# TensorE marks graph 1 through the two PSUM banks of the column codes, and a round's second one-hot is issued behind the logits' maxima

## What is computed

```
# layer 0: of each node the first 25 neighbours by column; their elementwise maximum
vals, idx = top_k(where(A != 0, -arange(N), -inf), 25)
agg = max over the valid of X[idx];  agg = where(degree <= 25, maximum(agg, 0), agg)
x = layernorm(x + relu(concat([X, agg]) @ W + b))
# layer 1: attention of 8 heads over the neighbours
Wh = x @ W1;  e = leaky(s1[i] + s2[j] + emb[adj])  where adj, else -1e9
h = softmax(e) @ Wh;  x = layernorm(x + elu(layernorm(h) * gamma + beta))
```

## Time and profile before

| what | us |
|---|---|
| median of 3 runs (lowest, highest) | 3056.82 (3050.93, 3058.76) |
| the profiled execution | 3059.63 |
| its span | 3057.9 |
| VectorE busy | 2525.2 (83%) |
| GpSimd busy | 2208.5 (72%) |
| TensorE matmuls busy | 2007.9 (66%) |
| ScalarE busy | 1058.5 (35%) |

### The profile page before, as it was taken

One profiled execution on the slowest core, in us unless ns is written; L12 is line 12 of the kernel. 1 busy time (PEld: TensorE's weight loads), 2 busy tenths in 40 slices (PEclk: granted clock), 3 DMA queues, 4 the chain that ended last, 5 costly groups with the idle time before them and its releaser, 6 DMA issues.

```text
span 3057.9 us, 30468 instructions
## 1 busy us (share of the span) xinstructions
PE 2007.9 (66%) x6994; PEld 1423.7 (47%) x6995; DVE 2525.2 (83%) x5841; ACT 1058.5 (35%) x2587; POOL 2208.5 (72%) x2341
## 2 busy tenths in 40 slices
PE   8247566756666667766667667676677666477565
PEld 1134344534444445544455545554455444356453
DVE  6798887998888988889889988889896866577676
ACT  4223224333333333333443333333432222234334
POOL 3475567777777777777777777777777777777774
PEclk9968778777877788888888888887897887689787
DMA  8877667656666666766676666676655554445443
GB/s 300 258 229 227 205 213 220 187 171 191 203 184 207 189 195 209 216 208 188 205 218 193 195 205 217 190 220 193 198 156 143 158 147 132 128 134 170 128 134 91
DMA packets 282490, 577.75 MB, mean 189 GB/s; under 512 B 68801, under 2 KB 192706, under 8 KB 265922
## 3 DMA queue, kind: packets, MB, share of 16 engines
q0 software_dynamic: 109824, 305.79, 36.0%
q1 hardware_dynamic: 172482, 269.96, 26.4%
HBM read 488.78 MB, written 86.77 MB: 188 GB/s over the span
## 4 chain that ended last, share of the span: by engine, by line
POOL 43%; issue 18%; DVE 15%; PE 6%; DVEq 3%; DMA 3%; ACT 2%; POOLq 0%; ACTq 0%; SPq 0%
POOL ring L706 43%; DVE agg L1353 3%; DVEq L1126 3%; DVE pay L1172 2%; PE att_p L1016 2%; PE lin_p L979 1%; DMA ring<-nat_d,idx 1%; DVE ring L1492 1%; DVE agg L1344 1%; DVE pick L1230 1%; DVE adj_h L1159 1%; DMA ring<-table_d,top 1%; POOL pair_s L714 1%; PE score_p L952 0%; DVE lst L1251 0%
## 5 line engine op out<-in xcount | busy, mean ns | idle before, releaser
L706 POOL DMA_INDIRECT ring<-nat_d,idx x1096 | 1052.1, 960 | 390.6 <-issue 355.4
L706 POOL DMA_INDIRECT ring<-table_d,idx x1096 | 1046.2, 955 | 346.9 <-issue 332.0
L1016 PE MATMUL att_p<-ring,ident 128*128 128x256 f32 (+1 forms) x2384 | 575.2, 397 | 211.3 <-ACT x_t L809 125.6
L1016 PEld LDWEIGHTS att_p<-ring,ident 128*128 128x128 f32 (+1 forms) x2384 | 461.9, 198 | 327.4 <-issue 180.7
L1353 DVE TENSOR_REDUCE agg<-ring 128x256 f32<-128x2560 f32 (+9 forms) x120 | 473.1, 3942 | 2.7 <-issue 0.4
L979 PE MATMUL lin_p<-w_s,h_t 128*128 128x256 f32 x1024 | 428.9, 592 | 0.0
L979 PEld LDWEIGHTS lin_p<-w_s,h_t 128*128 128x128 f32 x1024 | 289.3, 296 | 123.1 <-issue 65.1
L837 ACT ACTIVATE neg<-z 128x256 f32<-128x256 f32 x128 | 53.3, 416 | 799.0 <-DVE z L1395 799.0
L1492 DVE TENSOR_TENSOR ring<-ring,score_p 128x1536 f32<-128x1536 f32 (+10 forms) x128 | 320.6, 2504 | 10.3 <-issue 1.0
L966 PE MATMUL turn_p<-ident,xs 128*128 128x128 f32 x256 | 65.5, 346 | 383.1 <-ACT h_t L802 365.0
L952 PE MATMUL score_p<-pay,pick 128*128 128x323 f32 x896 | 299.2, 482 | 18.9 <-DVE pick L1230 16.2
(11 more groups left out here) (193 smaller groups left out, 2868.8 us busy)
## 6 DMA issues: line engine op xcount, KB each, us to landing
adj_i<-in_adj_dram SPq DMA_DIRECT2D x128, 1024.0 KB, 5.7
sorted_d<-srt SPq DMA_DIRECT2D x112, 161.5 KB, 2.8
ring<-nat_d,idx POOLq DMA_INDIRECT x1096, 2.9
ring<-table_d,idx POOLq DMA_INDIRECT x1096, 2.9
table_d<-tab SPq DMA_DIRECT2D x128, 132.0 KB, 4.4
nat_d<-pay SPq DMA_DIRECT2D x32, 514.0 KB, 4.6
pay<-in_x_dram SPq DMA_DIRECT2D x32, 512.0 KB, 7.5
xs<-sorted_d SPq DMA_DIRECT2D x128, 128.0 KB, 4.1
```

The lines of the kernel that those rows point to most:

```text
L706: pool.indirect_dma_start(out=to[:, k * width:(k + 1) * width], out_offset=None, in_=source, in_offset=bass.IndirectOffsetOnAxis(ap=idx_at ...
L1016: last = pe.matmul(att_p[:, 0:C], ident[0:on, :], r3[0:on, s, 0:C], start=(s == 0), stop=(s == k - 1))
```

## The change

Graph 1's tiles (n = 16 to 31) are marked by TensorE as graph 0's are. Their slices use only two banks, those that hold the column codes later (`score` for n >= 16: bank c % 2), so a slice waits until VectorE has taken the maxima of the slice two before it (`score_free`). In the steps 16 to 22 TensorE does the four slices of tile n at the head of its step, ahead of `ranks` and the permutes. In rounds 0 to 8, slices 2 and 3 of tile r + 23 stand between TensorE's first permute and `turn(r)`, slices 0 and 1 of tile r + 24 at the end of its round. VectorE takes the maxima of slices 0 and 1 where `chunks` stood and of 2 and 3 where `mark(n+1)` stood. `cast(n)` waits for `score_ready` up to n = 33. The column codes wait in `res`, and VectorE copies them to PSUM in four pieces in round 8, ahead of `mark(32)`, instead of one copy in step 16. The constants for TensorE's marks move out of `ring` to `fin` and `turned_out`. `index_rows` decodes graph 1 as graph 0. In all rounds the second `pick_rows` is issued behind the maxima of the logits; in rounds without logits, behind x1.

```diff
-        parts_h = ring[0:64, 2 * N:2 * N + N // 2].bitcast(BF16)
-        mark_h = ring[:, 3 * N:3 * N + P // 2].bitcast(BF16)
-        cols_h = x1k[:, 0:N // 2]
+        parts_h = fin[0:64, :].bitcast(BF16)
+        mark_h = turned_out[0][:, 0:P // 2].bitcast(BF16)
+        cols_h = [res[c][:, :] for c in range(4)]
...
-            return score_banks[(4 * n + c) % BANKS]
+            return score_banks[(4 * n + c) % BANKS if n < T else c % 2]
+
+        def score_free(n, c):
+
+            return 4 * n + c - BANKS + 1 if n < T else 4 * T if n == T and c < 2 else 4 * n + c - 1
...
-                if n < T + 2:
+                if n < 2 * T + 2:
                     need(act, score_ready, 4 * (n - 1))
                 else:
-                    need(act, cast_used, n - 1 - T)
+                    need(act, cast_used, n - 1 - 2 * T)
...
-            def mark(n):
+            def mark(n, quarters=range(4)):
 
                 pe.wait_ge(cast_done, n + 1)
-                for c in range(4):
+                for c in quarters:
                     at = slice(512 * c, 512 * (c + 1))
-                    need(pe, score_used, 4 * n + c - BANKS + 1)
+                    need(pe, score_used, score_free(n, c))
...
             for n in range(AHEAD):
-                if n < T:
-                    mark(n)
+                mark(n)
...
-            pe.wait_ge(score_used, 4 * T)
+            mark(AHEAD, (0, 1))
...
                 if perms:
                     permute(perms[0])
+                if r + AHEAD < 2 * T:
+                    mark(r + AHEAD, (2, 3))
...
                     if first(r):
                         turn(r)
+                if r + AHEAD + 1 < 2 * T:
+                    mark(r + AHEAD + 1, (0, 1))
...
-                if first(n):
+                if n < 2 * T:
+                    search_first(n, (0, 1))
+                elif first(n):
                     chunks(n)
                 if r and ranked_in(r - 1) is not None:
                     rank_rows(ranked_in(r - 1))
-                for x in PERMS_OF[r]:
-                    pick_rows(x)
+                perms = list(PERMS_OF[r])
+                if perms:
+                    pick_rows(perms[0])
...
                     v.tensor_reduce(mx[:, :], e3.rearrange("p k h -> p h k"), AX, ALU.max)
+                if perms[1:]:
+                    pick_rows(perms[1])
+                if first(j):
                     settle()
                     v.tensor_tensor(e3, e3, mx[:, :].unsqueeze(1).broadcast_to([P, k, H]), ALU.subtract)\
                         .then_inc(logits_ready, 1)
...
-                if first(n + 1):
+                if n < 2 * T:
+                    search_first(n, (2, 3))
+                if n + 1 == 2 * T:
+                    settle()
+                    for c in range(4):
+                        v.tensor_copy(score_p[0][:, C * c:C * (c + 1)], cols_h[c])
+                    settle()
+                if 2 * T <= n + 1 < TILES:
                     mark(n + 1)
...
-                    v.tensor_copy(score_p[0][:, :], cols_h)
```

More of the change, by code:

```diff
@@ L75 @@
 CONSTS1 = 45
-CONSTS = 48
+CONSTS = 51
 ORDER1 = [6, 14, 11, 0, 2, 4, 13, 15, 1, 3, 5, 8, 10, 7, 9, 12]
@@ L683, in _ @@
             step(pool.tensor_scalar(cols_i, cols_i, 65536.0, None, ALU.mult))
-            step(pool.tensor_copy(cols_h.bitcast(BF16), ring[:, 0:N]))
+            for c in range(4):
+                step(pool.tensor_copy(cols_h[c].bitcast(BF16), ring[:, 512 * c:512 * (c + 1)]))
             assert steps == CONSTS
@@ L1173, in chunks, with search_first @@
                 last.then_inc(cast_used, 1)
[L1175 to L1182, removed]
+            def search_first(n, quarters=range(4)):
+                if quarters[0] == 0:
+                    free_pay(n)
+                for c in quarters:
                     dve.wait_ge(score_ready, 4 * n + c + 1)
@@ L1243, in index_rows @@
                 i3 = idx_part(b, part)
-                none = 0.0 if b else MARK
+                none = MARK if b < 2 else 0.0
                 rounds = [-(-SLOTS[at + u] // 8) for u in range(PART)]
@@ L1272, in index_rows @@
                 settle()
-                if b == 0:
+                if b < 2:
                     v.scalar_tensor_tensor(l3, l3, none, l3, ALU.is_gt, ALU.mult)
@@ L1521, in _ @@
                     degree_codes(n // GROUP)
[L1522 to L1525, removed]
+                search_first(n)
                 if n % GROUP == GROUP - 1:
@@ L1531, in _ @@
                     score_weights()
-            mark(AHEAD)
             settle()
```

## The result

| kernel | median us (lowest, highest) | runs | ratio to before, 95% interval | span of the profiled execution |
|---|---|---|---|---|
| before | 3056.82 (3050.93, 3058.76) | 3 | | 3057.9 |
| after | 3102.37 (3100.80, 3102.61) | 3 | 1.015 (1.0136 to 1.0164) | 3100.9 |

A forecast was written before the change was run, and what follows sets the result against it. VectorE's chain up to GpSimd's first layer-1 gather at 446 us was taken to bound the kernel. 8.3 - 1.0 + 38 + 2 - 2.4 = +45, less a little, +44 us: 3100 us, range 3072 to 3124.

The forecast's parts named there:

- the gather: GpSimd's first gather of layer 1, at 446 us before; expected near 490 us after the change.
- the ring: Rounds 1 to 7: slices, cast, `h_t`, `turn`, linear and VectorE's maxima wait in a closed cycle through three engines; +38 us.
- What bounds the kernel: Up to 446 us VectorE's work stands end to end; a microsecond there moves GpSimd's first layer-1 gather and the end equally.
- VectorE's saving: Per tile of graph 1, VectorE's product goes and maxima come out of PSUM: 0.94 us less a round, if TensorE is never late.
- The terms of the ring: Rounds 1 to 7: TensorE fp32 66 us, slices 22.7, ScalarE's casts, copies and tables, VectorE 18.7; 123 us after overlap and clock.
- Steps 16 to 22: Before round 0: TensorE's slices delay the permutes from step 20 on, and VectorE waits; +8.3 us, or +5.5 with 0.54 us slices.
- The moved one-hot: The second one-hot, issued later, saves VectorE's waits for permutes in rounds 10 and 14; -2.4 us.
- Whatever happens on the other engines there is covered.: From 446 us on GpSimd never stands still, so delays on other engines cost nothing until the last 30 us.
- The hidden ring: Rival: the next tile's slices 0 and 1 are always ready when VectorE needs them; -10 us, 3047 us, chance 0.08.
- No change: Rival: the loss ahead of the first layer-1 gather doesn't reach the end; 3057 us, chance 0.10.
- The upper clock throughout: Rival: TensorE runs at its upper clock throughout, rounds 1 to 7 take 100 us; sum +19, 3076 us, chance 0.22.
- the lower clock throughout: Rival: TensorE runs at its lower clock throughout, rounds 1 to 7 take 149 us; sum +71, 3128 us, chance 0.10.

The follow-up runs named there:

- ring_open: The changed kernel with slices 2 and 3 at the head of TensorE's round and slices 0 and 1 of the next tile ahead of `turn`; 3052.49 us.
- all_early: ring_open with the two permutes of step 21 put behind TensorE's marks of step 22; 3049.05 us, 0.9974 of before.
- slices23_early: The changed kernel with only slices 2 and 3 at the head of TensorE's round; on two other chips 3859.06 us (0.9958 of before there) and 3919.43 us (0.9991).

## Why the prediction was right, point by point

| stretch | predicted | measured |
|---|---|---|
| to the start of round 0 | +8.3 | +2.9 (149.65 against 146.78) |
| round 0 | -1.0 | -0.8 |
| rounds 1 to 7 | +38 | +40.2 |
| round 8 | +2 | +2.2 (12.8 against 10.6) |
| rounds 9 to the gather | -2.4 | -2.1 |
| behind the gather | 0 to -0.5 | +0.6 |
| span | +44 to +45 | +43.0 |

The start of round 0 is +2.9 against before; against the two repeats of its steps it is +6.2 and +3.4. As a single stretch is known to 3 or 4 us, the agreement of the entries of about 2 us and less shows nothing. That the median came within 2.4 us of the forecast is in part luck too: the 5.4 us too much ahead of round 0 and the 2.2 too little in the ring, whose own terms missed in both directions, took each other off.

- **What bounds the kernel.** Right for what lies ahead of the gather, and the step that carried the most: six kernels and one bare delay moved the gather by 6 to 44 us, and the end moved with it, within the few us by which the last column varies.
- **VectorE's saving.** 0.94 us a round was predicted; VectorE's busy time fell by 1.00 a round in ring_open and in all_early, the two kernels whose rounds show it with hardly a wait on slices (by 0.82 in after, where the waits hide it).
- **The ring.** Its links are the ones named: the cast on slice 3, `h_t` behind the cast, `turn` on `h_t`, slice 0 behind linear. Opening any of them gave time back, opening it in two places gave all of it. The signs asked for came too: 41.6 us of waits for slices in the seven rounds (30 or more), 57.3 us before seven casts, where it was 18.8, the gather at 488.7 (near 490).
- **The terms of the ring.** The sum hit, its parts less so. TensorE's groups of after in these rounds (174.8 to 299 us), to be read beside the earlier trace rows:

```profile
L984 PE MATMUL lin_p<-w_s,h_t 128*128 128x256 f32 x56 | 25.6, 638 | 0.0
L957 PE MATMUL score_p<-pay,pick 128*128 128x323 f32 x64 | 25.1, 547 | 8.2 <-DVE pick L1234 8.2
L938 PE MATMUL score_p<-adj_h,turned_out 128*128 128x512 bf16 x26 | 11.0, 422 | 0.0
...
L982 PE MATMUL lin_p<-b_s,ones 1*128 1x256 f32 x14 | 8.5, 709 | 0.0
L971 PE MATMUL turn_p<-ident,xs 128*128 128x128 f32 x14 | 4.6, 434 | 22.0 <-ACT h_t L807 22.0
```

  The seven linears took 25.6 us, 3.66 each (3.40 to 3.78 in order of time), where 18.9 + about 3 had been counted. In before two of the seven took 1.99 us and five 3.6 to 3.8, those of rounds 1 and 6 too, which the forecast's list of slow ones (rounds 3, 4 and 7) leaves out. In after each came behind a pause of 2.8 to 3.5 us ahead of `turn`. With the bias matmuls (8.5 against 6.4) that is 6 us more than the term. The pauses ahead of `turn` were 22.0 us and hold the casts; the forecast had 10.6 for the copies, 13.4 for the casts and 1.4 for the tables, 25.4 together, so here it counted too much. The slices cost less than their term too: 21 on the ring were put at 22.7 us, less 6.5 for those behind permutes, so 16.2; in order of time nearly all of them took 0.64 us, behind permutes and elsewhere, and only five of 28 some 0.8 to 1.1: about 15. The forecast's clock ("mixed as now") was right in sum and not in its parts: slices mostly at the upper level (granted clock 1.00 from 264 to 265.5 us), linear at the lower (0.50 from 257.4 to 261).
- **Steps 16 to 22.** The step that failed: +8.3 was 5.4 too much (2 to 5 against the three traces with the steps of before). TensorE of after in order of time, from the end of the slices of step 20:

```profile
129.94 4.67 PE L957 MATMUL score_p<-pay,pick 128*128 128x323 f32 x8
135.25 2.42 PE L957 MATMUL score_p<-pay,pick 128*128 128x323 f32 x8 [0.64 <-issue]
137.51 0.38 PE L938 MATMUL score_p<-adj_h,turned_out 128*128 128x512 bf16 x1
137.82 0.39 PE L939 MATMUL score_p<-fin,ones_h 64*128 64x512 bf16 x1
```

  The permutes start at 129.94, not at 132.8, because the slices of tile 20 did not queue as worked out (the third waited 1.02 us for a bank, the fourth not at all); and from 137.51 on a slice costs 0.64 us (two at 0.32 from start to start) where 1.08 was taken. The text had 5.5 as its other end; the +2.9 lies below that too, though the repeats (+3.4 and +6.2) leave it open by how much.
- **The moved one-hot.** The -2.4 is not shown. The two pairs give -2.4 and -1.9 behind round 8, but the wait that was to shrink did not, and executions with the instructions of before differ by 2.4 us in this stretch (186.2 to 188.6). The agreement is luck.
- **"Whatever happens on the other engines there is covered."** Too strong. It holds for what this change does there (from the gather to the end 2612.2 against 2611.6), not for any delay: of 16.8 us in round 60 about 6 come through by the medians.
- **The rivals.** The hidden ring fell with 41.6 us of waits. "No change" fell with the gather, which came 42.4 us later, with nothing given back behind it. The upper clock throughout (3076) fell on linear; the lower clock throughout (3128) on the slices.

## What to carry to other kernels

When work moves from one engine into another's queue, write down who waits for whom from one round to the next: here each engine had time to spare, and the closed cycle through three queues cost 5.7 us a round. The same matmuls cost nothing that could be measured once they stood where their engine paused and ahead of the waits, so try the places in the queue before giving up the idea, and look at the in-order neighbours on the third engine first (the cast). And find the last point behind which a saturated engine hides everything, measure every variant up to that point, and test the cover with a bare delay, since it has an end. And take a second trace of the kernel before, before reading an effect of 2 us into a stretch: here the repeats alone differed by 3 to 4.

## What the runs showed of the hardware

**The step of a 512-column matmul.** With alternating weights it is 0.54 us from start to start in the first 88 us, though the granted clock reads 1.00 there, and 0.32 us behind fp32 permutes (137.51 to 137.82, above). TensorE's loads of the bf16 weights, same lines, in the seven rounds of after:

```profile
L938 PEld LDWEIGHTS score_p<-adj_h,turned_out 128*128 128x128 bf16 x26 | 2.7, 103 | 4.5 <-issue 3.9
```

The two steps are those of the two levels of the clock: in after the matmuls of the slices at 225.63 and 226.17 us follow each other at 0.54 us, where the granted clock of 224 to 227 us reads 0.52, and those at 264.12 and 264.43 us at 0.31 to 0.32, where that of 264 to 265.5 us reads 1.00. So the entry of 1.00 does not fit the matmuls of the first 88 us. It does not fit up to the first permute of step 20 in after either (4.67 us, the next one 2.42, both under an entry of 1.00). The Trainium skill ("TensorE: Matmul & The Clock Gate") gives 426.7 and 215.7 ns from start to start for 512 columns at the two levels (section "Wait — 56ns, not 53.3ns?"), and 128 / 1.2 = 107 ns for a load of 128 columns (section "LDWEIGHTS (loading the stationary operand)"). An estimate that adds the load to each is 533 and 322 ns, and the trace agrees with both, as it would with a load that isn't hidden behind the matmul. Its figure of about 131 ns for each 512-column matmul in a stream of loads and matmuls (section "Back-to-back issue gap") has no match in these rows.

**Chips with pauses.** On the two chips of the last four runs VectorE's instructions take as long as elsewhere (busy 2519.2 us in slices23_early, 2513.5 in after), but many start late. VectorE of slices23_early in order of time:

```profile
744.16 0.20 DVE L1500 RECIPROCAL su<-su 128x8 f32<-128x8 f32 x1 [0.96 <-issue]
745.57 0.25 DVE L1502 TENSOR_TENSOR score_p<-score_p,su 128x80 f32<-128x80 f32 x1 [1.21 <-issue]
746.96 2.82 DVE L1509 TENSOR_TENSOR ring<-ring,score_p 128x2560 f32<-128x2560 f32 x1 [1.14 <-issue]
```

VectorE stands some 1 us ahead of three instructions, for nothing that the profile shows, and the whole kernel takes 3859 us for the same work. The longer pauses come back at the same place: ahead of the maxima that open round 2 VectorE stands 16.78 us in slices23_early and 17.01 us in its repeat on the other chip. The cause is open.
